# A graph network block on one core: scatters of edge logits further behind the gathers, edge groups placed anew, graph softmax one output tile lower

## The reference

```python
def _L1_gnn_ref(x, edge_index, rms_w, W_down, Wl, Wr, att, W_up):
    x = x * rsqrt(mean(square(x)) + EPS) * rms_w
    x = x @ W_down                                   # 1024 -> 256
    src, dst = edges and one loop per node
    xl, xr = (x @ Wl).reshape(n, 4, 64), (x @ Wr).reshape(n, 4, 64)
    msg = xl[src] + xr[dst]                          # the two gathers
    act = where(msg > 0, msg, 0.2 * msg)
    e = einsum('ehd,hd->eh', act, att)               # the logits, 4 per edge
    m = segment_max(e, dst)
    p = exp(e - m[dst]); denom = segment_sum(p, dst)
    alpha = p / (denom[dst] + 1e-16)
    return segment_sum(alpha * xl[src], dst).reshape(n, 256) @ W_up

def _L1_mix_ref(x, Wq, Wk, Wv, Wo, bo, proj):        # 16 heads of 64
    q, k, v = heads of x @ Wq, x @ Wk, x @ Wv
    qp = ratio * (exp(q @ proj.T - |q|^2/2 - max over features) + EPS)
    kp = ratio * (exp(k @ proj.T - |k|^2/2 - max over all) + EPS)
    out = qp @ (kp.T @ v) / (qp @ sum(kp))
    return out @ Wo + bo
...
x = x + _L1_gnn_ref(xn, ...) + _L1_mix_ref(xn, ...)
x = x + _L1_ffn_ref(_layernorm(x), ...)
```

## Time and profile before

| | |
|---|---|
| median of 3 runs | 1727.08 us (1725.53 to 1733.59) |
| the profiled execution | 1727.72 us, span 1725.6 us, granted clock 0.987 |
| TensorE busy | 1667.9 us, 97% of the span |
| VectorE, GpSimd, ScalarE busy | 876.7, 666.8, 406.6 us |
| gathers and scatters of the edges (L1452, L1465) | 255 indirect DMAs, from 611.49 to 1072.66 us |
| attention's unit loop | about 840 to 1053 us |
| output projection and graph softmax | about 1059 to 1172 us |

### The profile page before, as it was taken

The page is one execution under the profiler, slowest core; times in us unless marked ns, Lnnn a source line. Parts: engine busy times, 40 slices in busy tenths (PEclk is TensorE's granted clock), DMA queues, the critical chain, the costliest instruction groups (busy, mean ns, idle before and its releaser), DMA issues. The chain is left out here.

```text
span 1725.6 us, 21020 instructions
## 1 busy us (share of the span) xinstructions
PE 1667.9 (97%) x7840; PEld 1036.1 (60%) x7840; DVE 876.7 (51%) x1721; ACT 406.6 (24%) x754; POOL 666.8 (39%) x535
## 2 busy tenths in 40 slices
PE   9999999999999998999989999998998999999998
PEld 6466446445444666655567775555676766776633
DVE  5887344562722565465355553867653222222337
ACT  1000000001411000001257772752101222122232
POOL 0566886220000067867788873000041322312213
PEclk9999999999999999999899999999999999999999
DMA  9655115453450044333322222724085999999951
GB/s 346 216 146 152 2 1 138 121 185 69 169 209 5 0 113 119 93 102 99 92 51 55 57 55 58 178 94 161 1 209 190 408 414 405 415 415 414 376 138 60
DMA packets 105692, 281.71 MB, mean 163 GB/s; under 512 B 61761, under 2 KB 71219, under 8 KB 93346
## 3 DMA queue, kind: packets, MB, share of 16 engines
q1 hardware_dynamic: 30691, 218.54, 34.5%
q0 software_dynamic: 67872, 50.79, 13.4%
q10 hardware_dynamic: 7052, 11.35, 2.1%
HBM read 250.37 MB, written 29.80 MB: 162 GB/s over the span
## 5 line engine op out<-in xcount | busy, mean ns | idle before, releaser
L1057 POOL DMA_INDIRECT table_d<-wring x85 | 179.0, 2106 | 107.8 <-issue 66.9
L1452 POOL DMA_INDIRECT wring<-xl_d,wring x85 | 114.9, 1352 | 247.7 <-DMA xr_d<-flat_b 221.8
L1465 POOL DMA_INDIRECT score_d<-wring x85 | 107.3, 1262 | 70.8 <-DMA score_d<-wring 50.0
L3127 PEld LDWEIGHTS bank<-picked_flat,wring 128*128 128x128 f32 x1152 | 129.4, 192 | 7.7 <-issue 7.7
L3127 PE MATMUL bank<-picked_flat,wring 128*128 128x128 f32 x1152 | 131.3, 276 | 0.0
L1452 POOL DMA_INDIRECT wring<-xr_d,wring x85 | 117.1, 1378 | 25.9 <-issue 25.3
L3134 PE MATMUL bank<-wring,picked_flat 128*64 128x256 f32 x640 | 74.9, 388 | 4.4 <-PEq L2601 4.4
L3239 PE MATMUL bank<-wring,region_a 128*125 128x512 f32 x160 | 70.6, 604 | 2.7 <-issue 2.7
L2213 DVE TENSOR_REDUCE q_top<-bank 125x1 f32<-125x266 f32 x80 | 34.7, 433 | 74.2 <-PE bank L1815 73.8
L1768 PE MATMUL bank<-wring,flat_d 128*125 128x512 f32 x160 | 71.4, 598 | 0.3 <-DVE flat_b L2162 0.3
L1653 PE MATMUL bank<-wring,region_a 128*125 128x512 f32 x160 | 70.3, 594 | 0.5 <-DVE region_a L1957 0.5
(11 more groups left out here) (494 smaller groups left out, 3147.3 us busy)
## 6 DMA issues: line engine op xcount, KB each, us to landing
wring<-in_experts SPq DMA_DIRECT2D x57, 2048.0 KB, 18.6
wring<-in_L_Ws SPq DMA_DIRECT2D x6, 2048.0 KB, 15.5
table_d<-eq_buf SPq DMA_DIRECT2D x2, 3072.0 KB, 28.2
score_d<-no_edge SPq DMA_DIRECT2D x2, 3072.0 KB, 33.1
wring<-table_d POOLq DMA_DIRECT2D x10, 610.4 KB, 7.3
wring<-score_d SPq DMA_DIRECT2D x5, 1093.8 KB
wring<-pid_d ACTq DMA_DIRECT2D x17, 312.5 KB
wring<-in_edge_w ACTq DMA_DIRECT2D x17, 312.5 KB
```

Of the source, the lines that this page charges most:

```text
L1057: pool.indirect_dma_start(out=tables_d[b % 2], out_offset=bass.IndirectOffsetOnAxis(ap=edge_at[:, b:b + 1], axis=0), in_=edge_sums[:, b, : ...
L1452: pool.indirect_dma_start(out=to[:, g % 2, j, :], out_offset=None, in_=table, in_offset=bass.IndirectOffsetOnAxis(ap=index[:, b:b + 1], ax ...
L1465: pool.indirect_dma_start(out=score_d, out_offset=bass.IndirectOffsetOnAxis(ap=cell_i[:, b:b + 1], axis=0), in_=logit[:, b, :], in_offset= ...
L3127: ins = pe.matmul(put(n), w[:, k * HALF + c * P:k * HALF + (c + 1) * P], picked_t[:, k, :], start=(k == 0), stop=(k == K - 1))
```

## The change

Five edits, all of order. (1) Scatters stand 14 blocks behind the gathers instead of 11; at blocks 64, 69, 74 and 79 the lag falls by one, with two scatters in a row there, so that ten are left at the end. (2) In the projections, the edge steps of groups 2 and 3 stand in key columns 1 and 2 (t2, t1, u3, c21 each), none in columns 0 and 3. (3) Group 8 stands after value tile 8, no longer in attention. (4) In attention, groups 9 to 16 start at u = 3, 13, 23, 34, 45, 56, 67 and 77; before, groups 8 to 16 started at 0, 7, 16, 27, 38, 48, 59, 69 and 80. (5) Turn, rows and up of the graph softmax stand one output tile lower; VectorE's maxima and weighing stay where they are. The table of early steps is cut here:

```diff
-        SCATTER_LAG = 11
         GB = 5
         GROUPS_E = EB // GB
+        SCATTER_LAG = 14
+        CATCH_UP = (64, 69, 74, 79)
...
-        V_GROUP_AT = {0: 4, 2: 5, 4: 6, 6: 7}
+        V_GROUP_AT = {0: 4, 2: 5, 4: 6, 6: 7, 8: 8}
...
-                       ("k", 0, "u3"), ("k", 0, "c21"), ("k", 1, "t2"), ("k", 1, "t1"),
...
+                       ("k", 1, "t2"), ("k", 1, "t1"), ("k", 1, "u3"), ("k", 1, "c21"),
...
-        LATE_STARTS = (0, 7, 16, 27, 38, 48, 59, 69)
-        LAST_START = 80
+        LATE_STARTS = (3, 13, 23, 34, 45, 56, 67)
+        LAST_START = 77
...
-        TURN_AT = {5: 0, 6: 1, 7: 2, 8: 3, 9: 4}
-        ROWS_AT = {6: 0, 7: 1, 8: 2, 9: 3}
+        TURN_AT = {4: 0, 5: 1, 6: 2, 7: 3, 8: 4}
+        ROWS_AT = {5: 0, 6: 1, 7: 2, 8: 3, 9: 4}
...
-        UP_AT = {7: 0, 8: 1, 9: 2}
+        UP_AT = {6: 0, 7: 1, 8: 2, 9: 3}
...
                 pe_gemm_rows(pe, k1_t, beside=attend)
-                up_product(T - 2)
-                gat_rows(T - 1)
                 up_product(T - 1)
...
-                for b in range(2 * GB, EB + SCATTER_LAG):
-                    if b < EB:
-                        gather_block(pool, b)
-                    if b >= SCATTER_LAG:
-                        scatter_block(pool, b - SCATTER_LAG)
+                scattered = 0
+                for b in range(2 * GB, EB):
+                    gather_block(pool, b)
+                    lag = SCATTER_LAG - sum(b >= at for at in CATCH_UP)
+                    while scattered <= b - lag:
+                        scatter_block(pool, scattered)
+                        scattered += 1
+                for b in range(scattered, EB):
+                    scatter_block(pool, b)
...
-                add_up(v, T - 2)
                 for t in range(T - 1):
```

## The result

The changed kernel took 1748.88 us (median of 4 runs, 1747.16 to 1754.12), the kernel before, measured beside it, 1727.09 us (4 runs). The ratio is 1.0124, 95% interval 1.0091 to 1.0158: slower by 21.8 us, where 10.9 were predicted. Side and order of events are as forecast; the size is twice as large and above the range. The profiled execution took 1754.12 us (span 1752.1), the longest of its four, 26.4 more than the profiled one of before.

What follows compares the result with a forecast made beforehand. TensorE was taken as the bound, busy 1667.9 of 1725.6 us, with gathers in GpSimd's queue setting VectorE's waits. 11.2 - 0.5 = +10.7 on 1727.72 gave 1738.4, stated as 1738, range 1727 to 1746 us.

Steps and rivals of the forecast that it cites:

- the landings from GpSimd's queue: Gathers for edge groups land 4.3 us after their start; lag 14 makes groups 3 to 12 land 4.6 us earlier.
- the new wait ahead of the queries: VectorE stands before group 9 from about 839 to 858.8, making the first query maximum 5.8 us later.
- The 8.0 us from the key projection: Moving group 2 to the second key column removes VectorE's 6.00 us wait and gains 8.0 us there.
- +11.2 us at the output projection: Unit 80 of attention comes at 1051.8 instead of 1040.63, delaying all that follows by 11.2 us.
- The term of the catch-ups: Four paired scatters wait 1.7 us each, one more scatter adds 1.5: group 16's last gather 8.3 us later.
- a wait costs itself and about 0.5 us: In attention, a VectorE wait costs TensorE its length plus about 0.5 us; read from 4.1 lost for 3.5 waited.
- The softmax steps (-0.5 us): Graph softmax one tile lower: the first turn waits for nothing, and 0.48 us before the last up product goes.
- the 3.1 us to spare: At the first turned probabilities: scaling ends at 1101.6, TensorE turns them at 1104.7.
- worse: Last scatters too late for the first turn of probabilities; two more held up give +6.5, 1744.9 us; chance 0.10.
- faster: Long scatter waits do not recur, group 9 lands near 837, VectorE waits nowhere: -17.4, 1710 us; chance 0.09.
- the round-robin rule: GpSimd's scatter waits, 9.60 us during weight loads against 0.30 else, would be no fixture; gathers could run ahead.
- Even: Catch-ups find their scatter landed and load waits shrink a little: +4.4 - 0.5, 1731.6 us; chance 0.21.

Runs made afterwards that it cites:

- e5: Kernel before with only the changed logit groups and early steps, scatters eleven behind and old softmax steps: ratio 1.0031.
- e10: Changed kernel without catch-ups and with the softmax steps at before's output tiles: ratio 1.0038.
- e15: The changed kernel itself, measured again: ratio 1.0100.
- e3: Changed kernel without catch-ups, scatters fourteen behind throughout: ratio 1.0061, 1743.01 us.
- e8: Changed kernel with the last logit group back at unit 80 instead of 77: ratio 1.0076.
- e1: Kernel before with scatters fourteen behind the gathers, no catch-ups, groups and softmax as before: ratio 1.0006.
- e2: Kernel before with scatters fourteen behind and the four catch-ups, groups and softmax as before: ratio 1.0015.
- e6: Changed kernel with the graph softmax's turn, rows and up steps back at before's output tiles: ratio 1.0125.
- e14: Kernel before with scatters fourteen behind, the four catch-ups, and the last group from unit 78 instead of 80: ratio 1.0082.
- e4: Kernel before with only the graph softmax steps one output tile lower: ratio 1.0030.
- e11: Kernel before with scatters fourteen behind, no catch-ups, and softmax steps one output tile higher: ratio 0.9996.
- e7: Kernel before with the last logit group started at unit 76 instead of 80: ratio 1.0020.
- e9: Kernel before with the last logit group from unit 75 and the one before it from 68: ratio 1.0029.
- e13: Changed kernel without catch-ups, softmax steps of before, last group from unit 72 and the one before it from 65: ratio 1.0066.
- e16: Kernel before with the last logit group from unit 74 and the one before it from 67: ratio 1.0059.

## Why the prediction was wrong

Up to g10 the times hold within 2 us: the landings from GpSimd's queue, the new wait ahead of the queries, the first maximum at 860. The 8.0 us from the key projection did not: 1.6 were left behind the wait at g3. That did not matter, because g9's landing sets what follows. e5 shows this part of the loss alone (0.31%), e10 with the scatters fourteen behind (0.38%). The sum was +11.2 us at the output projection; the profile has +26.1. Two differences make it up, 5.0 and 9.9 us.

**The term of the catch-ups was too small, by 5.0 us.** It was said that g16 lands 1031.57 + 4.3 + 8.3 = 1044.2; it started at 1049.2. The 8.3 were 12.9 for the catch-ups (four times 1.52 + 1.7) less 4.6 for the lag. In the changed kernel the gathers of block 64, the last ahead of the first catch-up, stand 3.8 us ahead of before's, and g16's last 13.2 us behind: the lead was 0.8 us short and the four added 17.0 us, 4.1 more than forecast (14.3 us in e15). Between e3 and the changed kernel, which differ in nothing else, the last gather moves by 15.0 us. The row of the tail gave the wait behind a scatter (1.99 us, measured 1.94 to 2.16), but not that the second scatter then takes 2.07 to 2.13 us for 1.21; behind the first of them two gathers also took 1.97 and 2.49 us for 1.22.

**The step "a wait costs itself and about 0.5 us" failed at g16, and cost 9.9 us.** It was read off g9, and holds there. The trace of before had a warning beside that row: from 867 to 871, just behind g9's start, its granted clock was 0.57, and the prediction did not look at it:

```profile
867.00:871.00 4.00, 3.81 (x18) 2.89 (x19) 1.24 (x3) 2.53 (x7) 3.39 (x3) 0.57 0.11 30
```

At g16, from VectorE's first instruction to the turned attention (L377) the forecast had 0.5 + 7.1 + 13.3 = 20.9 us; it took 28.0, and from there to the projection 8.1 instead of 5.2. Of these 36 us, 30.7 ran at the 1.2 GHz level. e8 takes the wait away by the group's place and e3 by its landing, and both times the half clock behind it goes and the projection comes 19.8 and 23.2 us earlier: it is shown that the changed kernel's stretch hangs on the last group's wait, and that this wait needs both edits. Why the clock stayed low so long stays open. That the parts don't add up says the same: the catch-ups cost 0.1% with the last group at unit 80 (e1 to e2) and 0.9%, some 15 us, with it at 77 (e10 to e6). Those two pairs differ in the other groups as well; e2 to e14 moves the last group alone, by two units, and costs 0.67%. The prediction priced the wait by its length and did not look at what the clock does behind it.

**The softmax steps (-0.5 us) were right for this kernel for a reason that the prediction did not weigh.** The probabilities were put at 23.8 us behind the last scatter; the six profiles whose first turn waited (e1, e3, e4, e8, e10, e11) have 23.4 to 23.8. But the 3.1 us to spare were in truth 6.2 (1119.6 less 1113.4, where ScalarE's scaling ended), only since the projection was later still. The scaling ended 28.2 us behind the last scatter there, as VectorE came to the scores at 1099.84, behind its work on the output tiles, and no longer waited for them. e4, and e3 beside e10, show what this edit costs when it isn't: 0.2 to 0.3%. The rival "worse" had the right mechanism, and it is what took back half of the repair in e8.

The 26.1 us are those of the profiled execution, which took 5.2 us more than its own median; the medians differ by 21.8. e15's profile had g16 at 1046.8, 23.9 us at half clock and the projection at 1079.0, +19.8: there the two differences are 2.6 and 6.1 us. So the split into 5.0 and 9.9 is of one execution, and part of the difference between executions is the length of this stretch.

The chances have a slip: at 1735.0, with two catch-ups that wait for nothing, the forecast would be just inside 0.5% (1735.7), not over it.

Of the rivals, "faster" needed g9 to land before 846.5: it started at 858.38. The scatters' long waits did recur (7.33, 8.36, 4.45, 2.28 and 2.46 us up to g9), so the round-robin rule that the prediction took from the Trainium skill (DMA: Bandwidth & Descriptors, section SWDGE vs HWDGE vs iDMA) did not decide this case. "Even" needed catch-ups that wait for nothing; each waited 1.94 to 2.16 us.

## What to carry to other kernels

A wait of TensorE is not priced by its own length alone: look at the granted clock behind waits in the profile, and reckon the work that follows at the low level. How long it lasts varied between executions of one kernel here, so read the mean clock of every execution, not of the profiled one alone. Two edits that make the same consumer early and its data late must be priced together, and tried apart. When transfers share one queue with those that a later stage waits for, moving some forward moves the others back: find the length of the chain behind the last one (here about 23.5 us) before counting a gain.

## What the runs showed of the hardware

- TensorE was at the 1.2 GHz level for 20.5 to 30.7 us around and behind waits of 5.2 to 5.5 us (changed kernel, e6, e14, e15), although it was busy over 85% of that time; with waits of 2.9 to 4.85 us (e2, e7, e9, e13, e16) it was 6.8 to 10.2 us. Elsewhere waits of 5.20 us (kernel before, key projection) and 5.59 us (changed kernel, g9) came with 6.8 and 10.2 us. The runs do not separate the length of the wait from the smaller stops ahead.
- In e7 three of 12 executions, in e9 one of 12, had a mean granted clock of 0.976 to 0.978 and took 1739.6 to 1746.4 us, the others 0.982 to 0.987 and 1726.7 to 1740.2 us. Where in them the low clock lay was not profiled.
- A second indirect scatter issued directly behind another waited 1.94 to 2.16 us and itself took 2.07 to 2.13 us instead of 1.21, in all four pairs of the changed kernel; in e15 one of the four took 1.21. In the tail, with no gathers beside them, eight of the ten took 1.19 us.
- In e4 a wait of 3.66 us at the first turned probabilities, after TensorE had been busy 13.8 of 16 us, came with 10.2 us at half clock; the edit that made it cost 0.3% (5 us).
